# A convolution, attention and MLP block on one core: the last image's post-processing is reordered, the band's rows are spread by matrix products, and the slots of all engines are redrawn

## The reference

```
# 1: group norm, softmax attention over 8 heads of 32, projection, residual
xn = group_norm(x); q, k, v = split(w_qkv @ xn + b_qkv)
x1 = x + w_proj @ softmax(q k / sqrt(32)) v + b_proj
# 2: linear attention on LayerNorm(x1) = t, 1024 tokens of 256
q, k = elu(t @ Wqk + bqk) + 1;  z = 1 / (q . mean(k) + 1e-6)
u = x1 + rope(q) @ (rope(k)^T t / n) * z + conv3(t) + lepe_b
# 3: MLP on the low band of a Haar transform of LayerNorm(u) = c
ll = sum of 2 x 2 blocks / 2; h = gelu(interp(ll) @ fc1^T + b1)
out = u + idwt(h @ fc2^T + b2, other bands of c)
```

## Time and profile before

| What | us |
|---|---|
| median of three runs (1381.51 to 1382.86) | 1381.69 |
| the profiled execution, whole | 1382.15 |
| its span | 1380.4 |
| TensorE busy (share of the span) | 1211.1 (88%) |
| VectorE busy | 991.3 (72%) |
| ScalarE busy | 881.9 (64%) |
| GpSimd busy | 465.6 (34%) |
| first exponential starts | 31.4 |
| last exponential starts | 1273.5 |

### The profile page before, as it was taken

The page is one execution under the profiler, slowest core; times in us unless marked ns, Lnnn a source line. Parts: engine busy times, 40 slices in busy tenths (PEclk is TensorE's granted clock), DMA queues, the critical chain, the costliest instruction groups (busy, mean ns, idle before and its releaser), DMA issues.

```text
span 1380.4 us, 21964 instructions
## 1 busy us (share of the span) xinstructions
PE 1211.1 (88%) x7868; PEld 629.9 (46%) x7868; DVE 991.3 (72%) x1607; ACT 881.9 (64%) x1457; POOL 465.6 (34%) x623
## 2 busy tenths in 40 slices
PE   6888899899988999899988999899998999878846
PEld 5544544545444454444445454444444444433433
DVE  2676688848887597857889487866889487874551
ACT  1667677576766667576776768676776767656402
POOL 2001017510384015720195014730176103830450
PEclk8999999999999999999999999999999999999977
DMA  8243324133433225233252224332341333300101
GB/s 267 54 119 73 91 63 108 48 70 97 109 76 92 54 67 132 57 75 103 67 120 71 53 81 124 60 92 71 89 112 53 69 90 84 81 31 16 46 17 46
DMA packets 51355, 111.28 MB, mean 81 GB/s; under 512 B 15504, under 2 KB 15760, under 8 KB 50992
## 3 DMA queue, kind: packets, MB, share of 16 engines
q1 hardware_dynamic: 48576, 100.85, 30.0%
q0 software_dynamic: 2480, 8.78, 2.0%
q10 hardware_dynamic: 192, 0.26, 0.1%
...
## 4 chain that ended last, share of the span: by engine, by line
PE 44%; DVE 29%; POOL 8%; ACT 8%; issue 6%; SPq 3%; DMA 2%; DVEq 0%; POOLq 0%; ACTq 0%
DVE negmax L1025 15%; PE ps_s L636 10%; PE ps_o L651 7%; ACT probs L887 6%; PE work L663 4%; PE work L710 4%; POOL x L1356 4%; PE work L724 4%; PE work L782 4%; DVE ln_st L1090 3%; DVE tok L1101 3%; PE work L787 3%; POOL csum L1353 1%; DVE t L1177 1%; DVE lo L1070 1%
## 5 line engine op out<-in xcount | busy, mean ns | idle before, releaser
L887 ACT ACTIVATE probs<-ps_s,negmax 128x1024 f32<-128x1024 f32 x512 | 569.7, 1113 | 322.2 <-DVE negmax L1025 314.9
L1025 DVE TENSOR_REDUCE negmax<-ps_s 128x1 f32<-128x1024 f32 x512 | 620.0, 1215 | 192.1 <-PE ps_s L636 189.6
L636 PE MATMUL ps_s<-q_st,k_st 128*128 128x512 f32 x1024 | 404.6, 478 | 59.4 <-ACT probs L887 49.3
L636 PEld LDWEIGHTS ps_s<-q_st,k_st 128*128 128x128 f32 x1024 | 164.8, 191 | 285.5 <-ACT probs L887 167.0
L651 PE MATMUL ps_o<-probs,v_scaled 128*32 128x512 f32 x2048 | 248.8, 603 | 2.8 <-POOL v_scaled L1297 2.8
L1297 POOL TENSOR_TENSOR v_scaled<-v_tok,rsums 128x128 f32<-128x128 f32 x128 | 51.2, 400 | 545.0 <-DVE rsums L1031 544.2
L663 PE MATMUL work<-xg,w_qkv 128*128 128x512 f32 x256 | 119.6, 592 | 0.0
L724 PE MATMUL work<-ln_ch,w_qk 128*128 128x512 f32 x236 | 113.8, 604 | 2.1 <-DVE k_ch L1203 2.1
L651 PEld LDWEIGHTS ps_o<-probs,v_scaled 128*32 128x32 f32 x2048 | 53.7, 109 | 127.0 <-issue 119.8
L1356 POOL TENSOR_TENSOR x<-x,csum 128x1024 f32<-128x1024 f32 x45 | 106.8, 2373 | 2.0
L887 ACT ACTIVATION_READ_ACCUMULATOR probs<-ps_s,negmax 128x1 f32 x512 | 99.1, 194 | 0.0
...
## 6 DMA issues: line engine op xcount, KB each, us to landing
q_st<-hi SPq DMA_DIRECT2D x128, 128.0 KB, 2.4
q_st<-lo SPq DMA_DIRECT2D x120, 128.0 KB, 2.4
...
k_st<-hi SPq DMA_DIRECT2D x128, 64.0 KB, 2.0
k_st<-lo SPq DMA_DIRECT2D x128, 64.0 KB, 2.0
x<-in_x SPq DMA_DIRECT2D x8, 1024.0 KB, 4.8
...
xg<-in_x POOLq DMA_DIRECT2D x7, 1024.0 KB, 5.7
```

Source lines behind the costliest of these rows:

```text
L636: mm = pe.matmul(ps_s[s % 2][:, half * HALF:half * HALF + HALF], k_st[:, h, j * P:j * P + P], q_st[g][:, h, half * HALF:half * HALF + HALF ...
L887: act.activation(probs[:, j % 2, h, :], ps_s[s % 2][:, :], ACT.Exp, bias=negmax[:, s % 4:s % 4 + 1], accum_out=sums[:, j % 2, h:h + 1]).th ...
L1025: dve.tensor_reduce(negmax[:, s % 4:s % 4 + 1], ps_s[s % 2][:, :], AX_X, ALU.max, negate=True)\
```

## The change

1. **Prologue.** 11 and 11 dummies in place of 8 and 20.
2. **Slots.** All tables are redrawn, most by one to three slots. `add_norm` becomes a step of its own (`add`). In the last image the band's step on VectorE goes to slot 63. SyncE does `half_turn0` before `keys1`, `late_store` before `late_keys0`, and `residual` behind `keys0` (middle images) or behind `spread` (last image).
3. **Tail, MLP.** A step of `fc2` waits for its own two Gelus alone, and the steps stand between those of `fc1`; `ll` waits for the pair sums two token blocks at a time.
4. **Tail, rows.** The band's rows are spread by two products with a constant matrix (`rows`), loaded in the tail, and `up` reads PSUM; the four transfers go.
5. **Tail, rotary.** The cosine and the sum of the second group (`late_turn`) go from GpSimd to VectorE; semaphores of the rotary are split by group.
6. **Tail, dummies.** 28 steps of two dummies, into the PSUM of the softmax output. The three taps on VectorE stand ahead of all Elus.

```diff
 PE_TAIL = {
-    "fc2": (60, 60, 60, 60),
...
+    "warm": (14, 15, 16, 16, 16, 16, 16, 16, 16, 16, 16, 16, 32, 32, 32, 32, 32, 32, 32, 32, 33, 33, 39, 43, 44, 44, 44, 44),
+    "fc2": (52, 59, 60, 60), "denT": (32,), "rows": (63, 63), "lnT": (8, 8, 14, 14),
...
-            "fc2": (band_done, 1, lambda n: 1), "rT": (r_ch_done, 4, lambda n: 1 + n),
+            "fc2": (band_done, 1, lambda n: 1), "rows": (out_done, NC, lambda n: 1 + n), "rT": (r_ch_done, 4, lambda n: 1 + n),
...
             elif n in (2, 4):
+                eng.wait_ge(q_turned[g], 2 * HG * DMA * (b + 1))
                 eng.wait_ge(made["den"], b + 1)
-                eng.tensor_tensor(q_ch[:, g, :], q_ch[:, g, :], const("cos_ch"), ALU.mult).then_inc(turn_step, 1)
+                eng.tensor_tensor(q_ch[:, g, :], q_ch[:, g, :], const("cos_ch"), ALU.mult).then_inc(turn_step[g], 1)
             else:
-                eng.wait_ge(turn_step, 4 * b + 3 + g)
+                eng.wait_ge(turn_step[g], 2 * (b + 1))
...
             def epilogue():
+                sp.wait_ge(made["w1"], 2)
+                sp.dma_start(con[:, SPREAD:SPREAD + P], consts[:, CONST_W:CONST_W + P]).then_inc(spread_in, DMA)
...
                 elif name == "ll":
-                    pe.wait_ge(csum_done, 4 * (b + 1))
                     for nb in range(NB):
+                        if nb % 2 == 0:
+                            pe.wait_ge(csum_done, 4 * b + nb // 2 + 1)
...
                 elif name == "fc2":
-                    pe.wait_ge(gelu_done, 8 * (b + 1))
+                    pe.wait_ge(gelu_done, 8 * b + 2 * n + 2)
...
+                elif name == "rows":
+                    pe.wait_ge(band_done, b + 1)
+                    half = slice(LL // 2 * n, LL // 2 * n + LL // 2)
+                    pe.wait_ge(spread_in, DMA)
+                    pe.matmul(ps[:, :], con[half, SPREAD:SPREAD + P], band[half, :], start=True, stop=True)\
+                      .then_inc(made[name], 1)
...
                 pe.wait_ge(const_in, CONST_LOADS)
-                warm_up(8)
+                warm_up(11)
...
                     if tile[0] == "gn":
-                        warm_up(20)
+                        warm_up(11)
...
                     dve.wait_ge(r_ch_done, 4 * (b + 1))
-                    dve.wait_ge(band_spread, 4 * DMA * (b + 1))
+                    if b == B - 1:
+                        dve.wait_ge(made["rows"], n + 1)
+                        spread = bank(("rows", n))
+                    else:
+                        dve.wait_ge(band_spread, 4 * DMA * (b + 1))
+                        spread = band_rows[:, n, :]
...
-                    if kind == "epilogue":
-                        add_norm(dve, b, n)
+                elif name == "add":
+                    add_norm(dve, b, n)
...
-                elif name == "turn":
-                    turn_q(dve, b, n)
+                elif name == "late_turn":
+                    turn_q(dve, b, n + 4)
...
+    spread = (p[:, None] % (P // 2) == p[None, :] // 2).astype(np.float32)
```

127 lines of the change are left out of this document (70 added, 57 removed), and 30 rows, old and new, of tables (ACT_STEADY, DVE_LAST, DVE_STEADY, PE_STEADY).

## The result

Four executions of the changed kernel took 1368.03 us in the median (1364.11 to 1371.81), four of the kernel before beside them 1381.92. The ratio is 0.990, with a 95% interval of 0.987 to 0.993. The forecast was 1366.5, and faster. The execution that was profiled is the fastest of the four, 1364.11 (span 1362.3), so it is set against the profiled 1382.15 of before (span 1380.4). That makes 18.0 us in all, 4 more than the medians give (13.9).

The account below looks back on a forecast made before the run. The loop over heads was taken as bound by TensorE, the tail as waits counting in full; 1382.15 - 2.0 - 3.0 - 1.2 - 9.0 = 1366.95, or 1366.5 on the median's scale, range 1359 to 1377.

Parts of the forecast that it names:

- Prologue, -2.0: Start of the kernel: fewer dummies let the first K projection start at 14.1 instead of 16.19; gain 1.0 to 2.1 us.
- Middle images, -3.0: Six middle images: 0.5 us each from TensorE's 1.79 us wait for the second rotary product; bounds -7.8 to +3.6.
- a change of more than 1.3 us an image: Sign of being wrong, middle images: 1.3 was the whole 1.79 us rotary wait, rounded down.
- The rival that redrawn slots do nothing: Loop over heads (9%): bound by TensorE, so the six images give 0; 1369.5 us.
- Last image, -1.2: Last softmax image: VectorE's 1.25 us wait for the fourth normalisation's root shrinks; bounds 0 and -2.4.
- Tail, -9.0: From the last projection to the last sums: legs together -9.1, taken as -9; bounds -11.5 and -6.
- first rotary product: Tail, on VectorE: at 1330.0 instead of 1330.90; as a sign, 1 us earlier against the projections' start.
- rows -3.1 (-3.3): Tail's end: two products replace four transfers, band to first sum 1.1 us instead of 4.40; -3.3.
- the 6 that I had set as a sign of being wrong: Tail, projections to last sum: wrong if it shrinks by less than 6 or more than 11.5 us.
- The tail keeps little: Rival (10%): full VectorE-GpSimd exclusion and dummies on the path; tail gives 3, loop and last image nothing; 1376.7 us.
- keep the clock: Rival (12%), tail: dummies hold TensorE at 2.4 GHz from the first LayerNorm transposes on; 4.0 less, 1362.5 us.
- The slower case: Rival (6%), middle images' start: VectorE waits 3.3 us for the band spread behind the residual; 20 us, 1386.5.

Follow-up runs that it names:

- steady_tied: Changed kernel with the middle images' tables and SyncE's order from the kernel before, each late addition right behind its pair sum: 1376.2 us, ratio 0.995.

## Why the prediction was right, and where it was not

**The sum: right by luck in part.** The forecast of 1366.5 for the median was met by 1368.0, with -2.0, -3.0, -1.2 and -9.0 where the profiles have -1.3, +5.9, -8.8, -3.3 and -10.5. These are of one execution each, the fastest of four after the change; over all profiles with the stretch unedited, against the one of before, they are -0.9 to -2.4, +5.1 to +8.7, -8.9 to -16.4, -2.4 to -3.3 and -4.9 to -10.5. (The low ends of my bounds sum to 23.8 us, not 23; it changes nothing.)

**Prologue, -2.0: right in the step, short by 0.7.** The first K projection starts at 14.02 (14.1 forecast), the stacking is 2.1 us earlier, and its landing takes the rest:

```profile
9.83 4.20 PE L848 MATMUL ps_s<-con 128*128 128x128 f32 x22
14.02 7.29 PE L680 MATMUL work<-xg,w_qkv 128*128 128x512 f32 x16
...
28.07 0.73 PE L653 MATMUL ps_s<-q_st,k_st 128*128 128x512 f32 x2 [3.08 <-DMA q_st<-hi]
```

The same wait before:

```profile
29.41 0.73 PE L636 MATMUL ps_s<-q_st,k_st 128*128 128x512 f32 x2 [2.32 <-DMA q_st<-hi]
```

TensorE waits 3.08 us for the stacked queries instead of 2.32. Over the profiles the first exponential comes at 29.0 to 30.5, so -0.9 to -2.4.

**Image 0: the step that failed is that there was none.** I priced six middle images, the last one and the tail, and left out the first image, whose tables were redrawn too. It costs 5 to 9 us; the old tables give 133.2 again.

**Middle images, -3.0: the mechanism right, the size not.** The term was 0.5 us an image for the second rotary product's wait. It measured 1.5 between the first two profiles and 1.8 to 2.8 against steady_tied: that wait gave 1.1, and the smaller waits around it, for the band's copy, the key means and exponentials, which I had not added up, are shorter by about the rest. I had said that a change of more than 1.3 us an image would prove me wrong, and it does. The rival that redrawn slots do nothing is out: steady_tied, whose interval (0.993 to 0.997) meets neither of the changed kernel's.

**Last image, -1.2: half of the gain seen.** The fourth root's wait is gone as said; the term was short by the 2.0 us at unit 31.

**Tail, -9.0: right in size, measured -10.5 in the profile,** inside the bounds of -11.5 and -6, and -7.5 in the mean of the seven profiles. By legs: first rotary product 2.15 us sooner (0.9 forecast); the half turn was issued 1.5 us sooner, not 0.8 later, but GpSimd took it up at the same point as before, behind its tap; to the pair sums 13.6 (13.8); ll ends 1.5 behind the last pair sum (1.0); from the last pair sum to the end of the MLP 17.0 (17.1); rows -3.1 (-3.3). But 96.4 is the shortest of the seven: with all the dummies the tail goes up to 102.0, a gain of 4.9 and so less than the 6 that I had set as a sign of being wrong. What I had no term for is the stop for a packet (0.9 us in the one, 2.4 in the other), the dummies' price at half clock, which I took at full clock (2.6), and the MLP at a lower clock (1.4).

**Rivals.** The tail keeps little: out, since even the longest of the seven gives 4.9 us and not 3, but the exclusion between VectorE and GpSimd is real, 2.0 us gained of 4.4. The dummies don't keep the clock: it is 0.54 over the 8 us around the start of the pair sums (64 to 72 us after the last exponential), and ll takes 3.65 us for its 16 matmuls as before. The slower case didn't come: the spreading, issued from 476.36 to 478.79 behind the residual, was in time, and VectorE went on with the first late sum when its maximum was done.

```profile
483.89 1.22 DVE L1224 SCALAR_TENSOR_TENSOR ln_ch<-csum,ln_ch 128x1024 f32<-128x1024 f32 x1
```
